# Attention and mixture-of-experts block on one core: turning four tiles of probabilities of the largest units on VectorE in blocks of 32, with the blocks exchanged through DRAM

## The reference, cut to what matters

```python
k = einsum('ihd,bpd->biph', W_K, x)     # x: 1 x 2048 x 512, 16 heads of 128
q = einsum('ihd,bpd->biph', W_Q, x)
v = einsum('ihd,bpd->biph', W_V, x)
scores = einsum('biph,biqh->biqp', k, q)
masked = scores * mask - 1e10 * (1 - mask)
attn = softmax(masked / sqrt(128), axis=-1)
z = einsum('biqp,biph->biqh', attn, v)
out = einsum('df,bqf->bqd', W_O, z_flat)
```

## Time and profile before

| | us |
|---|---|
| median of 3 runs | 2522.81 (2514.16 to 2532.49) |
| the profiled execution, its own time | 2530.3 |
| its span | 2528.5 |
| PE busy | 2440.2 (97%) |
| DVE busy | 1731.5 (68%) |
| ACT busy | 1436.3 (57%) |
| POOL busy | 350.9 (14%) |

### The profile page before, as it was taken

The page is one execution under the profiler, slowest core; times in us unless marked ns, Lnnn a source line. Parts: engine busy times, 40 slices in busy tenths (PEclk is TensorE's granted clock), DMA queues, the critical chain, the costliest instruction groups (busy, mean ns, idle before and its releaser), DMA issues. The chain is left out here.

```text
span 2528.5 us, 40864 instructions
## 1 busy us (share of the span) xinstructions
PE 2440.2 (97%) x14202; PEld 2119.3 (84%) x14202; DVE 1731.5 (68%) x3651; ACT 1436.3 (57%) x3217; POOL 350.9 (14%) x366
## 2 busy tenths in 40 slices
PE   6999999999999999999999999899999999999993
PEld 5888888888888888888888888688888989899993
DVE  4666666567567557567566576678748878788885
ACT  4555455455456446456455455555437767677774
POOL 0000000000000000000000000167621222221221
PEclk9999999999999999999999999999999999999997
DMA  7421411420331321322232133278649999999997
GB/s 266 133 64 57 141 59 49 131 78 28 124 105 28 128 72 59 126 68 66 88 104 66 55 121 111 81 276 317 221 129 306 306 292 305 280 306 311 304 311 213
DMA packets 193421, 397.01 MB, mean 157 GB/s; under 512 B 23673, under 2 KB 73209, under 8 KB 182976
## 3 DMA queue, kind: packets, MB, share of 16 engines
q1 hardware_dynamic: 165760, 334.89, 39.3%
q0 software_dynamic: 27456, 59.51, 9.9%
HBM read 296.45 MB, written 106.48 MB: 159 GB/s over the span
## 5 line engine op out<-in xcount | busy, mean ns | idle before, releaser
L514 ACT ACTIVATE pT_hi<-turned 128x512 fp32r<-128x512 f32 (+3 forms) x640 | 334.6, 535 | 267.8 <-PE turned L763 266.0
L503 ACT ACTIVATE probs<-bank,neg_max 128x512 f32<-128x512 f32 (+3 forms) x640 | 397.1, 627 | 109.4 <-DVE neg_max L613 104.3
L619 DVE TENSOR_TENSOR pT_lo<-turned,pT_hi 128x512 fp32r<-128x512 f32 (+3 forms) x640 | 377.6, 603 | 72.2 <-ACT pT_hi L514 68.8
L605 DVE TENSOR_REDUCE max_part<-bank 128x1 f32<-128x512 f32 (+2 forms) x576 | 345.5, 621 | 95.8 <-PE bank L746 83.8
L733 PE MATMUL bank<-x_sb,w_hi 128*128 128x512 f32 x1024 | 323.4, 397 | 20.2 <-ACT ident_bf L479 13.4
L763 PE MATMUL turned<-ident,probs 128*128 128x128 f32 x2176 | 329.2, 273 | 0.1
L763 PEld LDWEIGHTS turned<-ident,probs 128*128 128x128 f32 x2176 | 264.3, 141 | 49.0 <-PE bank L722 0.3
L778 PE MATMUL z_ps<-pT_hi,v_hi 128*128 128x512 f32 (+3 forms) x640 | 255.1, 399 | 3.5 <-DVE pT_lo L619 3.0
L746 PE MATMUL bank<-k_lo,q_hi 128*128 128x512 f32 (+2 forms) x640 | 254.3, 397 | 0.0
L746 PE MATMUL bank<-k_hi,q_hi 128*128 128x512 f32 (+2 forms) x640 | 253.3, 396 | 0.0
L1901 DVE TENSOR_TENSOR up_lo<-w_raw,up_hi 128x704 fp32r<-128x704 f32 x256 | 217.2, 886 | 46.9 <-ACT up_hi L1388 46.4
(11 more groups left out here) (206 smaller groups left out, 5158.5 us busy)
## 6 DMA issues: line engine op xcount, KB each, us to landing
w_raw<-in_w SPq DMA_DIRECT2D x256, 352.0 KB, 5.6
x_sb<-x_parts SPq DMA_DIRECT2D x62, 1024.0 KB, 6.1
w_raw<-in_w SPq DMA_DIRECT2D x128, 256.0 KB, 5.4
rows_in<-gathered_x SPq DMA_DIRECT2D x64, 263.5 KB, 5.7
spread_sb<-inv_dram POOLq DMA_DIRECT2D x64, 256.0 KB, 3.5
z_dram<-z_sb SPq DMA_DIRECT2D x64, 256.0 KB, 2.3
z_raw<-z_dram SPq DMA_DIRECT2D x16, 1024.0 KB, 5.1
w_raw<-in_w_qkv SPq DMA_DIRECT2D x32, 384.0 KB, 8.5
```

The costliest lines, as they stand in the source:

```text
L503: nc.scalar.activation(probs[:, u % 2, r, kc * CHUNK:kc * CHUNK + used], bank[:, job_at["s", h, c, r, kc] % BANKS, 0:used], ACT.Exp, bias= ...
L514: nc.scalar.activation(pT_sb[0][:, n % TURNS, lo_col:], turned[:, n % TURNS, lo_col:], ACT.Copy).then_inc(turn_hi, 1)
L605: nc.vector.reduce_max(max_part[:, row % ROWS, kc:kc + 1], bank[:, job % BANKS, 0:used], axis=AX_X).then_inc(part_done, 1)
L619: nc.vector.tensor_tensor(pT_sb[1][:, n % TURNS, lo_col:], turned[:, n % TURNS, lo_col:], pT_sb[0][:, n % TURNS, lo_col:].bitcast(F32), AL ...
```

## The change

Tiles `j` = 4 to 7 of both units with `c` = 3 (`FAR`), eight tiles of each pair and 64 in all, are no longer turned by TensorE. In their place there is a new step `b` (`blocks`), eight of them in the `ORDER`; apart from them the string is as before:

- VectorE, once the exponentials of row block 3, key chunk 1 of the unit are there, turns the tile of 128 by 512 with one instruction in blocks of 32 by 32 into `stage` (two slots). It reads `probs` at a step of four elements in its innermost dimension. It waits for the store of the tile two before.
- SyncE stores `stage` to a slot of `far_dram` (two slots in use); before it overwrites a slot it waits for the fetch of that slot's last content.
- GpSimd waits for the store and fetches the tile with the blocks exchanged, as pieces of 512 bytes, back to its place in `probs`.
- ScalarE's copy and VectorE's subtract of such a tile read `probs` in SBUF in place of `turned` in PSUM.

The columns of a turned tile now come in the order (quad, row block, 32). So that all tiles agree, the other transposes write their slot in four runs of 32 columns, the diagonal tiles are read and accumulated in four runs, and the final multiply takes its operands in the new order. To make room, `spread_sb` and `z_sb` have one slot in place of two: the spread of unit `u` waits for the result of unit `u - 1`, and a result waits for the store of the one before.

The diff, cut to its core:

```diff
+FAR = {3: range(4, 8)}
...
+        "b": [("blocks", 0, *tile) for tile in tiles if tile[2] in FAR.get(tile[1], ())],
...
+    FAR_SLOTS = 2
+    BLOCK = 32
...
-        spread_sb = sb("spread_sb", [P, 2, CHUNK], F32)
-        z_sb = sb("z_sb", [P, 2, CHUNK], F32)
+        spread_sb = sb("spread_sb", [P, CHUNK], F32)
+        z_sb = sb("z_sb", [P, CHUNK], F32)
+        stage = sb("stage", [P, 2, CHUNK], F32)
...
+        def by_quad(ap, first=0):
+            return ap.rearrange("p (a m) -> p a m", a=QUADS)[:, :, first * BLOCK:]
+        def far_place(h, c, j):
+            return probs[:, unit_at[h, c] % 2, :, j * P:(j + 1) * P]
...
+            def spread(i, u):
+                wait_apart(pool, waited, z_done, upto(i, n_units, u - 1))
...
+            def fetch(i, h, c, j):
+                m = far_at[h, c, j]
+                slot = m % FAR_SLOTS
+                wait_apart(pool, waited, far_out[slot], far_count(i, m, 16))
+                pool.dma_start(far_place(h, c, j), far_dram[slot].rearrange("(a j) (b m) -> (j b) a m", a=QUADS, b=QUADS)
+                               ).then_inc(far_in[slot], 16)
...
+                    if step[0] == "blocks":
+                        m = far_at[step[2:]]
+                        slot = m % FAR_SLOTS
+                        sp.wait_ge(blocks_made, i * n_far + m + 1)
+                        if i or m >= FAR_SLOTS:
+                            sp.wait_ge(far_in[slot], far_count(i, m - FAR_SLOTS, 16))
+                        sp.dma_start(far_dram[slot], stage[:, m % 2]).then_inc(far_out[slot], 16)
...
+                if (h, c, j) in far_at:
+                    act.wait_ge(far_in[far_at[h, c, j] % FAR_SLOTS], far_count(i, far_at[h, c, j], 16))
+                else:
+                    act.wait_ge(turn_ready, upto(i, n_near, near_at[h, c, j]))
...
+            def blocks(i, h, c, j):
+                m = far_at[h, c, j]
+                dve.wait_ge(exp_done, upto(i, n_exp, exp_at[h, c, RPC - 1, j // RPC]))
+                if i or m >= 2:
+                    old = (m - 2) % n_far
+                    dve.wait_ge(far_out[old % FAR_SLOTS], far_count(i if m >= 2 else i - 1, old, 16))
+                nc.vector.transpose(stage[:, m % 2].rearrange("p (b r n) -> p r b n", b=QUADS, r=RPC),
+                                    probs[:, unit_at[h, c] % 2, :, j * P:(j + 1) * P].rearrange(
+                                        "p r (n b) -> p r b n", b=QUADS)).then_inc(blocks_made, 1)
...
             def turn(i, h, c, j):
+                if (h, c, j) in far_at:
+                    return
...
-                    mark = nc.tensor.transpose(turned[:, n % TURNS, r * P:(r + 1) * P],
+                    mark = nc.tensor.transpose(by_quad(turned[:, n % TURNS])[:, :, r * BLOCK:(r + 1) * BLOCK],
                                                probs[:, u % 2, r, j * P:(j + 1) * P], ident[:])
```

More of the change, by code:

```diff
@@ L204, in attention @@
     turn_at, pv_at, unit_at = counted("turn"), counted("pv"), counted("out")
+    far_at = counted("blocks")
+    near_at = {tile: n for n, tile in enumerate(tile for tile in turn_at if tile not in far_at)}
+    n_far, n_near = len(far_at), len(near_at)
+    FAR_SLOTS = 2
+    BLOCK = 32
+    QUADS = P // BLOCK
+    assert n_far % FAR_SLOTS == 0
     assert counted("inverse") == unit_at
@@ L282, in attention @@
         waited = sem("waited1")
+        blocks_made = sem("blocks_made")
+        far_out = [sem(f"far_out{n}") for n in range(FAR_SLOTS)]
+        far_in = [sem(f"far_in{n}") for n in range(FAR_SLOTS)]
         z_done = sem("z_done")
@@ L319, in attention, with far_count, turned_tile, turned_parts @@
         pieces_after_job = {job: x_pieces[DT + n * per_job:DT + (n + 1) * per_job] for n, job in enumerate(early)}
+        def by_quad(ap, first=0):
+            return ap.rearrange("p (a m) -> p a m", a=QUADS)[:, :, first * BLOCK:]
+        def far_count(i, m, each):
+            return each * (i * n_far // FAR_SLOTS + m // FAR_SLOTS + 1)
+        def far_place(h, c, j):
+            return probs[:, unit_at[h, c] % 2, :, j * P:(j + 1) * P]
+        def turned_tile(h, c, j):
+            if (h, c, j) in far_at:
+                return far_place(h, c, j)
+            return by_quad(turned[:, turn_at[h, c, j] % TURNS], max(0, j - RPC * c))
+        def turned_parts(part, h, c, j):
+            return by_quad(pT_sb[part][:, turn_at[h, c, j] % TURNS], max(0, j - RPC * c))
+        def last_of(at, h, c, j):
+            before = [tile for tile in at if turn_at[tile] <= turn_at[h, c, j]]
+            return at[max(before, key=lambda tile: turn_at[tile])] if before else -1
+        def wait_turned(eng, i, h, c, j):
+            if last_of(near_at, h, c, j) >= 0:
+                eng.wait_ge(turn_ready, upto(i, n_near, last_of(near_at, h, c, j)))
+            far = [tile for tile in far_at if turn_at[tile] <= turn_at[h, c, j]]
+            last_far = max((turn_at[tile] for tile in far), default=-1)
+            if last_far < 0:
+                last_far = max(turn_at[tile] for tile in far_at) - n_turns
+            if upto(i, n_turns, last_far) > 0:
+                eng.wait_ge(turn_lo, upto(i, n_turns, last_far))
         def proj_dst(part, job):
@@ L362, in spread @@
                 wait_apart(pool, inv_free, inv_stored[u % 2], i * per + 16 * (u // 2 + 1))
-                wait_apart(pool, waited, z_done, upto(i, n_units, u - 2))
-                pool.dma_start(spread_sb[:, u % 2], inv_dram[u % 2:u % 2 + 1].to_broadcast([P, CHUNK])
+            def spread(i, u):
+                wait_apart(pool, waited, z_done, upto(i, n_units, u - 1))
+                pool.dma_start(spread_sb[:], inv_dram[u % 2:u % 2 + 1].to_broadcast([P, CHUNK])
                                ).then_inc(spread_in[u % 2], 16)
+            def fetch(i, h, c, j):
[4 more added lines that the diff above has]
+                               ).then_inc(far_in[slot], 16)
             def body(i):
+                passed = []
                 for step in plan:
                     if step[0] == "inverse":
-                        spread(i, *step[2:])
+                        store_inverse(i, *step[2:])
+                    if step[0] in ("inverse", "out"):
+                        passed.append((step[0], unit_at[step[2:]]))
+                        for u in range(n_units):
+                            if passed[-1] in (("inverse", u), ("out", u - 1)) and ("inverse", u) in passed and (
+                                    u == 0 or ("out", u - 1) in passed):
+                                spread(i, u)
+                    if step[0] == "blocks":
+                        fetch(i, *step[2:])
             for i in range(PAIRS):
@@ L667, in body @@
                             first_wo_lo(wo_lo_group[step[2:]])
+                    if step[0] == "blocks":
+                        blocks(i, *step[2:])
                     if step[0] == "inverse":
@@ L777, in value @@
                 for a, b in PASSES:
-                    mark = nc.tensor.matmul(z_ps[:, first * P:], v_sb[a][:, j, h * DH:(h + 1) * DH],
-                                            pT_sb[b][:, n % TURNS, first * P:],
+                    mark = nc.tensor.matmul(by_quad(z_ps[:], first), v_sb[a][:, j, h * DH:(h + 1) * DH],
+                                            turned_parts(b, h, c, j),
                                             start=(j == 0 and (a, b) == PASSES[0]),
```

43 lines of the change are left out of this document (21 added, 22 removed).

## The result

The changed kernel takes 2580.6 us against 2520.8 us in the same comparison: ratio 1.021, 95% interval 1.018 to 1.024. It is slower by 2.1%, outside the range that I gave. Its profiled span is 2578.8 us against 2528.5.

What follows compares the result with a forecast made beforehand. TensorE was taken to bound the attention (busy 1513.5 of 1520 us). Terms of +16.0, -12.3 and +4.0 summed to +7.7 us on the 2522.8 us median: 2530.5 us, no measurable change, range 2507 to 2562.

Steps and rivals of the forecast that it cites:

- Edits at nothing: Side edits priced at 0: single `spread_sb`, far tiles read from SBUF, runs of 32, the final multiply's step of 16 bytes.
- the price of a tile: TensorE time per tile of four transposes removed: 0.36 us plus 0.08 us at the matmul behind, 0.44 us in all.
- A turn: The new VectorE transpose of one far tile: 1.08 us like the line 639 multiply, 1.0 us worked with, 0.6 lower bound.
- the walk at (0,3): VectorE's steps followed in order: turns delay lo 8, 10, 11; TensorE loses 3.3 us, gets 1.3 back, balance +2.0 a unit.
- The last unit's +4.0: Unit (1,3) of the last pair, without projections as cover: +4 us once, bounds -2 and +8.
- The sum for the far tiles: 8 x 2.0 at (0,3), 7 x -1.75 at (1,3), last unit +4.0: +7.7 us.
- covered by 2.5 and 1.2 us, at nothing, and by little: Way through DRAM at (0,3): tiles 6 and 7 land that long before ScalarE needs them, so priced at 0.
- A: Rival: VectorE's idle takes all turns and TensorE keeps its 28 us: 2495 us; chance 0.10, in full or mostly.
- B: Rival: fetches at (0,3) take 6.2 us, not 3.5, and land late; 4.1 us a pair, 2563 us; chance 0.15.
- C: Rival: the VectorE turn itself takes over 1.5 us; each 0.5 us more costs about 12 us, 2550 us; chance 0.12.
- D: Rival: writing PSUM in runs of 32 slows TensorE's 1920 remaining transposes by 0.05 us each: 98 us, 2629 us; chance 0.03.

## Why the prediction was wrong

**What failed.** One term of "Edits at nothing": the single slots, taken at 0 in the sum. They measured +38 us by the medians, 1.7% by the ratio. The prediction has the single `spread_sb` fit, since "the two closest results, (0,0) and (1,0), have eight score blocks of three matmuls between them, over 5.5 us ... and the fetch takes 4.0. If that cover were gone it would cost under a microsecond a pair." It failed in two ways.
- It priced the spread near the median of the earlier trace rows. The transfer that counts is the one of (1,0), and the single slot itself moves its issue behind x, zeros and weights, where it takes 7.8 to 10.7 us (with one `spread_sb`, first seven pairs). The cover was longer than the 5.5 us (the two results start 9.1 us apart), and still too short. A median over 64 transfers says nothing on the one that is issued into a full queue. The timeline of SyncE before the change shows what is issued at that place.
- It left out the other half of the same edit, the single `z_sb`: the result of a unit now waits until the store of the one before has landed. It is in the diff and in my own description of it, and has no term in the sum. The trace before the change has that store of (0,0) at 8.5 to 10.3 us in seven pairs. Alone it cost 0.8%, the spread 0.35%.

**What came behind it.** The prediction had no term for the clock: every wait of TensorE is priced at its own length. The lower level follows the stall at (1,0) in all of the first seven pairs (9 us at (0,1)) and the waits at (1,2) in five of them (some 6 us at (1,2) and (0,3)). That is about 15 of the 55 us.

**What was right.** The bound is TensorE, and a tile is worth 0.44 us: unit (1,3) gave 1.7 us a pair for 1.75 (the second part of the price of a tile reads 0.07 and not 0.08 in the earlier trace rows, which changes nothing). A turn was worked out at 1.08 us (measured 1.09), the fetch at 3.5 (3.5). In the walk at (0,3), 3.3 us were to be lost at (1,2) and 3.1 were; 1.3 were to be got back and 1.1 were, in the run with that unit alone; so the balance was +2.0 worked out and +2.1 measured, where the clock stays up. Where it was lost, in front of values 8, 10 and 11, the timeline of TensorE of the changed kernel shows:

```profile
1216.84 0.47 PE L875 MATMUL z_ps<-pT_hi,v_hi 128*128 128x512 f32 x1 [0.51 <-DVE pT_lo L699]
...
1220.69 0.39 PE L875 MATMUL z_ps<-pT_hi,v_hi 128*128 128x256 f32 x1 [0.67 <-DVE pT_lo L699]
...
1223.06 0.33 PE L875 MATMUL z_ps<-pT_hi,v_hi 128*128 128x128 f32 x1 [1.30 <-DVE pT_lo L699]
```

These are idle times of 0.51, 0.67 and 1.30 us in front of the values of tiles 8, 10 and 11, against 0.6, 1.1 and 1.6 worked out. They add up to 2.5 us, not to the 3.3 of the walk nor to the 3.1 of the distance; no view shows the remaining 0.6 as idle time, so the agreement of the sums is in part luck.

**What was off in the far tiles.** The last unit's +4.0 was too much: the last pair is 0.5 us longer with the tiles of (1,3) alone, 3.4 with those of (0,3) alone, 3.7 with both. So (1,3) costs under 1 us there, and (0,3) more than the +2.0, since it gets nothing back. The sum for the far tiles was +7.7 us; the run with two slots shows +16 (0.6%). The last pair took +3.7 where +6.0 (2.0 and 4.0) had been worked out, and the first +1.7. The six inner pairs are 8.3 us longer in all, where the +0.3 of the undisturbed ones in each would be 2. The rest is one late fetch with the lower clock behind it (3.8 us), which I had as "covered by 2.5 and 1.2 us, at nothing, and by little", and the lower clock behind the waits at (1,2) in two more. Another 2.5 us lie ahead of the first result, where the change does nothing; kernels with other changes show 1.5 to 3.2 there, and the cause is open.

**The rivals.** A (VectorE hides it) is right for (1,3) alone. B (late fetch): in the changed kernel no row shows ScalarE waiting for a fetch. With two slots it occurs in one pair, where it costs 3.8 us with the clock, by a fetch of 4.8 us behind a store of 3.5; the median fetch takes 3.5 us and not 6.2. C and D are out. The mechanism that decided, a transfer that gets on the critical path since its buffer lost a slot, was none of them.

## What to carry to other kernels

A buffer that goes from two slots to one to make room is an edit of its own, with a price of its own. For each wait that it adds, look in the timeline of the queue at what is issued ahead of that one transfer, at the place where the two users stand closest; the median landing is no bound. Ask as well whether the new wait moves the issue of a transfer behind others. When the loss is large, measure the side edit by itself first: here it was two thirds to four fifths of the result, and moving the zeros and the loads of weights behind the store gave it back with no memory at all. A new instruction on an engine of 64% average costs nothing or twice its gain, by whether the stretch and the step behind it have slack. And before a difference between pairs is put down to a late transfer, look at the granted clock of that stretch.

## What I had not expected of the hardware

TensorE, idle for 4.5 us, ran its next 3.5 us at a granted clock of 0.51 (0.42 us between starts for 0.23), so the stall cost about a quarter more than its length. Short waits can have the same consequence: idle times of 0.5, 0.7 and 1.3 us at (1,2) were followed by the lower clock in five of the first seven pairs of the changed kernel and not in the other two, with the same instructions and the same idle times. With one `z_sb` an idle time of 1.8 us was followed by it, and one of 2.2 us was not. So from the length of an idle time these runs do not tell whether the clock falls. Writing PSUM in runs of 32 columns cost TensorE nothing: 273 ns in both kernels.
